# The last phase of a split-fp32 matrix product rewritten as a second Strassen step over pairs of samples, with part of its sums on GpSimd

## The reference, cut to what matters

```
y   = conv1d(x, weight, groups=4, pad=4) + (cond @ c_weight.T)[:, :, None] + bias   # x: (32, 128, 2048)
out = x + y @ kernel + ffn_bias                                                     # kernel: 2048 x 2048
        + B_eff (A_eff y) + B_shared (A_shared y)                                   # rank 32 each, mixed by gate
```

## Time and profile before

| | us |
|---|---|
| median of 3 runs | 1692.22 |
| lowest and highest | 1692.02, 1692.98 |
| the profiled execution's own time | 1692.59 |
| its span in the profile | 1690.8 |
| PE busy in it | 1680.7 (99%) |
| DVE busy | 1092.4 (65%) |
| ACT busy | 681.5 (40%) |
| POOL busy | 36.7 (2%) |

### The profile page before, as it was taken

The page is one execution under the profiler, slowest core; times in us unless marked ns, Lnnn a source line. Parts: engine busy times, 40 slices in busy tenths (PEclk is TensorE's granted clock), DMA queues, the critical chain, the costliest instruction groups (busy, mean ns, idle before and its releaser), DMA issues.

```text
span 1690.8 us, 21782 instructions
## 1 busy us (share of the span) xinstructions
PE 1680.7 (99%) x8432; PEld 1437.2 (85%) x8432; DVE 1092.4 (65%) x1501; ACT 681.5 (40%) x862; POOL 36.7 (2%) x70
## 2 busy tenths in 40 slices
PE   9999999999999999999999999999999999999998
PEld 6799998888888898888998888888888888888887
DVE  7888888965454689999986344455555545464443
ACT  7776776744222665566642112232233111121110
POOL 0011111110000000000000000000000000000000
PEclk9999999999999999999999999999999999999999
DMA  8978777976666667777666665577676898886764
GB/s 253 282 229 291 254 240 257 325 251 220 224 211 222 207 225 276 275 266 264 245 234 246 221 223 199 197 230 250 229 230 220 306 331 299 309 314 241 261 234 153
DMA packets 180287, 420.25 MB, mean 249 GB/s; under 512 B 50740, under 2 KB 90260, under 8 KB 175544
## 3 DMA queue, kind: packets, MB, share of 16 engines
q1 hardware_dynamic: 169960, 380.95, 65.9%
q0 software_dynamic: 9216, 33.56, 5.6%
q10 hardware_dynamic: 1008, 4.34, 0.9%
HBM read 272.76 MB, written 146.03 MB: 248 GB/s over the span
## 4 chain that ended last, share of the span: by engine, by line
PE 97%; DVE 2%; ACT 0%; DMA 0%; issue 0%; DVEq 0%
PE acc L1518 71%; PE cps L1387 15%; PE cps L1437 4%; PE acc L1421 3%; PE acc L1354 2%; PE acc L1471 1%; PE cps L1447 0%; DVE w_lo L975 0%; DVE x_q L986 0%; PE cps L1457 0%; PE acc L1493 0%; DMA st<-in_L_ffn_kernel 0%; DVE g L1012 0%; PE cps L1455 0%; DVE g L1003 0%
## 5 line engine op out<-in xcount | busy, mean ns | idle before, releaser
L1518 PE MATMUL acc<-w_hi,y_t 128*128 128x512 f32 x3584 | 991.7, 390 | 2.0 <-issue 1.0
L1518 PEld LDWEIGHTS acc<-w_hi,y_t 128*128 128x128 f32 x3584 | 665.3, 188 | 136.6 <-issue 2.1
L1518 PE MATMUL acc<-w_lo,y_t 128*128 128x512 f32 x1792 | 552.9, 390 | 0.0
L1518 PEld LDWEIGHTS acc<-w_lo,y_t 128*128 128x128 f32 x1792 | 336.3, 188 | 71.5
L713 ACT COPY x_q<-x_raw 32x512 f32<-32x512 f32 x248 | 269.6, 1087 | 21.1 <-DVE x_lo L993 13.4
L1387 PE MATMUL cps<-cw,x_hi 128*128 128x256 f32 (+2 forms) x1088 | 243.9, 312 | 0.4 <-DVE x_lo L1172 0.4
L752 ACT CAST y_t<-g 128x1024 fp32r<-128x1024 f32 x95 | 100.2, 1054 | 331.7 <-PE acc L1518 298.2
L1113 DVE TENSOR_TENSOR g<-acc,g 128x1024 f32<-128x1024 f32 x96 | 117.3, 1223 | 163.8 <-PE acc L1421 114.3
L1073 DVE TENSOR_TENSOR y_t<-g,y_t 128x1024 fp32r<-128x1024 f32 x95 | 116.1, 1222 | 102.0 <-ACT y_t L752 101.7
L1387 PE MATMUL cps<-cw,x_lo 128*128 128x384 f32 (+2 forms) x768 | 180.9, 283 | 0.0
L1387 PEld LDWEIGHTS cps<-cw,x_hi 128*128 128x128 f32 x1088 | 176.4, 189 | 3.6 <-DVE x_lo L1172 1.2
(11 more groups left out here) (127 smaller groups left out, 1006.6 us busy)
## 6 DMA issues: line engine op xcount, KB each, us to landing
g<-A SPq DMA_DIRECT2D x80, 512.0 KB, 4.7
g<-U SPq DMA_DIRECT2D x80, 512.0 KB, 6.2
A<-g SPq DMA_DIRECT2D x64, 512.0 KB, 4.6
g<-in_x SPq DMA_DIRECT2D x64, 512.0 KB, 6.2
out<-g SPq DMA_DIRECT2D x64, 512.0 KB, 3.5
x_raw<-in_x SPq DMA_DIRECT2D x31, 1024.0 KB, 5.2
U<-g SPq DMA_DIRECT2D x48, 512.0 KB, 4.1
g<-in_L_ffn_kernel POOLq DMA_DIRECT2D x32, 512.0 KB, 6.5
```

Of the source, the lines that this page charges most:

```text
L1518: ins = T.matmul(acc[:, b, m, :], y_buf[b][:, c, part, :], wt[:, k % SLOTS, m * 512:(m + 1) * 512], start=(c == 0 and part == 0 and wt is ...
```

## The change

Phase 6 is no longer 16 units but 8 passes over two pairs each (`one_pass`). In a pass the two units' products, 2 x (128 x 1024) by 1024 x 1024, are taken as one 2 x 2 block product, with the halves of K (512) as inner blocks and the halves of the columns (512) as outer ones, by a second Strassen-Winograd step: seven products of 128 x 512 by 512 x 512, each 12 matmuls (4 chunks by 3 split products) into one PSUM bank. The low-rank part is 2 matmuls for each of the four output blocks. A pass has 84 + 8 matmuls, where two units have 96 + 8.

- The weight of phase 6 (B22) becomes seven 512 x 512 blocks (14 tiles of 128 x 1024 where there were 8), three of them quarters of B22 and four formed from them: GpSimd loads B22, does 16 additions of 128 x 512 and stores `V4` to `V7` after the last convolution, in phase 3. The 14 tiles use `w_hi`/`w_lo` slots and the memory of `x_hi`, `x_lo` and `cw`, which nothing else uses by then. Six are split in phase 5, one in every one or two units, the other eight in its last unit and in the first pass.
- The seven left operands are a11, a12, a22 and four sums of the two samples' halves (`pass_sums`, four DVE instructions). Each is split apart (`hi_part`, `lo_part`, 128 x 512), in five buffers `y_part`.
- Of the products, P1 and P5 are copied out by ACT (`pass_copy`), P6 and P7 are added to running sums by DVE (`pass_us`), and GpSimd adds these four to the output tile: six additions of 128 x 512. GpSimd also does what `pre_add` did, two additions of 128 x 1024 (`pass_residual`). DVE adds the four banks that hold only their own block (`pass_add`), and SP stores each block of 256 KB apart.
- DMA issues of a pass are in another order (below). Unit 95, the last of phase 5, has its own low-rank part inside it, after chunk 6.

The core of the diff:

```diff
+EV_P1, EV_P2, EV_P6, EV_L11, EV_P5, EV_P7, EV_L22, EV_P3, EV_L12, EV_P4, EV_L21 = range(1, 12)
+EVS = 11
+EV_OF = (EV_P1, EV_P2, EV_P6, EV_P5, EV_P7, EV_P3, EV_P4)
+SUMS = (("E1", 0, 0), ("U2", 0, 1), ("P5", 0, 1), ("P5", 1, 1), ("U3", 1, 1), ("U3", 1, 0))
+SUMS_E1, SUMS_U2, SUMS_P5, SUMS_P5B, SUMS_U3B, SUMS_U3 = range(1, 7)
+ADDS = ((EV_L11, 0, 0, SUMS_E1), (EV_L22, 1, 1, SUMS_U3B), (EV_L12, 0, 1, SUMS_P5), (EV_L21, 1, 0, SUMS_U3))
+NADD = len(ADDS)
...
+        pair_w = [(w_hi[:, k], w_lo[:, k]) for k in (4, 5, 6)] + [
+            (xh_flat[:, k * HALF:(k + 1) * HALF], xl_flat[:, k * HALF:(k + 1) * HALF]) for k in range(2)] + [
+            (cw_flat[:, 0:HALF], cw_flat[:, HALF:2 * HALF])] + [(w_hi[:, k], w_lo[:, k]) for k in (7, 8, 9, 10, 0, 1, 2, 3)]
+        y_part = [cw_flat[:, 2 * HALF:3 * HALF].rearrange("p (c h o) -> p c h o", h=2, o=P)] + [
+            y_t[:, b, h * 4:(h + 1) * 4] for b in range(2) for h in range(2)]
...
+        part_src = [y_in_buf[0][:, 0:512], y_in_buf[0][:, 512:HALF], s_two, s_one, s_one, s_two,
+                    y_in_buf[1][:, 512:HALF]]
+        V1, V3 = B22[0:4][:, :, 0:512], B22[4:8][:, :, 512:HALF]
+        V2 = B22[4:8][:, :, 0:512]
+        PAIR_SRC = [V1, V2, V6_d, V5_d, V7_d, V3, V4_d]
+        pass_bank = {EV_P1: cps[:, 0, :], EV_L11: cps[:, 1, :], EV_P6: cps[:, 2, :], EV_P5: cps[:, 3, :],
+                     EV_P7: acc[:, 0, 0, :], EV_L22: acc[:, 0, 1, :], EV_L12: acc[:, 1, 0, :], EV_L21: acc[:, 1, 1, :]}
+        pass_out = [[g[:, 6], g[:, 0]], [g[:, 7], g[:, 1]]]
...
+            def load_pass_out(q, j):
+                u = QU + 2 * q + j
+                p = u % NP
+                if q == 0:
+                    sp.wait_ge(pre_added, lora_index(u) - 1)
+                else:
+                    sp.wait_ge(pass_pre, 2 * (q - 1) + j + 1)
+                sp.dma_start(xres[j], x[2 * p][:, HALF:L]).then_inc(xres_in[j], 16)
+                if q >= 2:
+                    sp.wait_ge(stage_out[j], 16 * (QU // 2) + 32 * (q - 1))
+                elif j == 0:
+                    sp.wait_ge(stage_out[q], 16 * (QU // 2))
+                else:
+                    sp.wait_ge(u4_out[q], 16 * (NP // 2))
+                sp.wait_ge(u4_out[p % 2], 16 * (p // 2 + 1))
+                sp.dma_start(pass_out[q % 2][j], U4_d[p]).then_inc(stage_in[j], 16)
+            def load_pass_y(u):
+                q, j = divmod(u - QU, 2)
+                if j == 0:
+                    sp.wait_ge(sums_ready, 4 * q)
+                    sp.wait_ge(y_lo_ready, QU + 7 * (q - 1) + 2)
+                else:
+                    sp.wait_ge(y_lo_ready, QU + 7 * q)
+                sp.dma_start(y_in_buf[j], A12_d[u % NP]).then_inc(y_in[j], 16)
+                sp.wait_ge(diff_ready, diff_index(u) - 1)
+                sp.dma_start(other[j], S2_d[u % NP]).then_inc(other_in[j], 16)
+            def store_pass(q, n):
+                j, h = ADDS[n][1:3]
+                sp.wait_ge(pass_added, NADD * q + n + 1)
+                sp.dma_start(out[2 * (2 * q + j)][:, HALF + h * 512:HALF + (h + 1) * 512],
+                             pass_out[q % 2][j][:, h * 512:(h + 1) * 512]).then_inc(stage_out[j], 16)
...
+            load_b(QU)
+            for j in range(2):
+                load_pair(10 + j)
+                load_pass_out(0, j)
+            for q in range(QS):
+                u = QU + 2 * q
+                if q >= 1:
+                    store_pass(q - 1, 3)
+                if q + 1 < QS:
+                    load_pass_y(u + 2)
+                for j in range(2):
+                    if q == 0:
+                        sp.wait_ge(lora_done, lora_index(u + j) - 1)
+                    else:
+                        sp.wait_ge(pass_ev, EVS * (q - 1) + (EV_L12, EV_L21)[j])
+                    sp.wait_ge(axd_out, 16 * NP)
+                    sp.dma_start(ax_words[:, j], axs_d[(u + j) % NP]).then_inc(axs_in[j], 16)
+                if q == 0:
+                    for n in (12, 13):
+                        load_pair(n)
+                    sp.wait_ge(evac_u, NP)
+                    sp.dma_start(U4_d[NP - 1], u2_buf[1]).then_inc(u4_out[1], 16)
+                    store_stage(QU - 1)
+                if q + 1 < QS:
+                    for j in range(2):
+                        load_pass_out(q + 1, j)
+                    load_pass_y(u + 3)
+                store_pass(q, 0)
+                if q + 1 < QS:
+                    load_b(u + 2)
+                store_pass(q, 1)
+                store_pass(q, 2)
+            store_pass(QS - 1, 3)
...
+            def pass_residual(q):
+                for j in range(2):
+                    pool.wait_ge(stage_in[j], 16 * ((QU + 2 * q + j - NP) // 2 + 1))
+                    pool.wait_ge(xres_in[j], 16 * (lora_index(QU + 2 * q + j) // 2 + 1))
+                    V.tensor_tensor(pass_out[q % 2][j], pass_out[q % 2][j], xres[j], ALU.add).then_inc(pass_pre, 1)
+            pass_residual(0)
+            for q in range(QS):
+                for n, (what, j, h) in enumerate(SUMS):
+                    half = pass_out[q % 2][j][:, h * 512:(h + 1) * 512]
+                    if what in ("E1", "P5"):
+                        pool.wait_ge(pass_copied, 2 * q + (1 if what == "E1" else 2))
+                    else:
+                        pool.wait_ge(pass_u, 2 * q + (1 if what == "U2" else 2))
+                    if n == 0:
+                        pool.wait_ge(pass_pre, 2 * q + 2)
+                    else:
+                        pool.wait_ge(pass_summed, len(SUMS) * q + n)
+                    V.tensor_tensor(half, half, pass_sum_buf[what], ALU.add).then_inc(pass_summed, 1)
+                if q + 1 < QS:
+                    pass_residual(q + 1)
...
+            hi_part(0)
+            split_pair(6)
+            hi_part(1)
+            split_pair(7)
+            hi_part(2)
+            split_pair(8)
+            for q in range(QS):
+                n = 7 * q
+                b_split(QU + 2 * q)
+                if q == 0:
+                    hi_part(3)
+                    split_pair(9)
+                hi_part(n + 4)
+                pass_copy(q, "E1")
+                if q == 0:
+                    split_pair(10)
+                    split_pair(11)
+                hi_part(n + 5)
+                if q == 0:
+                    split_pair(12)
+                    split_pair(13)
+                hi_part(n + 6)
+                if q + 1 < QS:
+                    hi_part(n + 7)
+                pass_copy(q, "P5")
+                if q + 1 < QS:
+                    for i in range(8, 11):
+                        hi_part(n + i)
...
+            lo_part(0)
+            split_pair(6)
+            lo_part(1)
+            difference(QU + 1)
+            pass_sums(0, 0)
+            split_pair(7)
+            lo_part(2)
+            pass_sums(0, 1)
+            pre_add(QU - 1)
+            split_pair(8)
+            for q in range(QS):
+                n, u = 7 * q, QU + 2 * q
+                more = q + 1 < QS
+                if q >= 1:
+                    pass_add(q - 1, 3)
+                b_split(u)
+                if q == 0:
+                    lo_part(3)
+                    pass_sums(0, 2)
+                    split_pair(9)
+                lo_part(n + 4)
+                if q == 0:
+                    split_pair(10)
+                    split_pair(11)
+                    evac_u4(QU - 1)
+                lo_part(n + 5)
+                if q == 0:
+                    split_pair(12)
+                    split_pair(13)
+                lo_part(n + 6)
+                if more:
+                    difference(u + 2)
+                pass_us(q, "U2")
+                if q == 0:
+                    evac(QU - 1)
+                pass_add(q, 0)
+                if more:
+                    lo_part(n + 7)
+                    lo_part(n + 8)
+                    difference(u + 3)
+                pass_us(q, "U3")
+                if more:
+                    pass_sums(q + 1, 0)
+                    lo_part(n + 9)
+                    pass_sums(q + 1, 1)
+                pass_add(q, 1)
+                if more:
+                    lo_part(n + 10)
+                    pass_sums(q + 1, 2)
+                pass_add(q, 2)
+            pass_add(QS - 1, 3)
...
+            def pass_product(q, i, ev, joined=False):
+                n = 7 * q + i
+                pe.wait_ge(y_lo_ready, QU + n + 1)
+                for c in range(NCH // 2):
+                    k = 2 * i + c // 2
+                    if q == 0:
+                        pe.wait_ge(w_lo_ready, NCH * 6 + k + 1)
+                    cols = slice(c % 2 * 512, (c % 2 + 1) * 512)
+                    for part, h in ((0, 0), (0, 1), (1, 0)):
+                        ins = T.matmul(pass_bank[ev], y_part[n % YS][:, c, part, :], pair_w[k][h][:, cols],
+                                       start=(c == 0 and part == 0 and h == 0),
```

(45 more changed lines are left out.)

191 lines of the change are left out of this document (164 added, 27 removed).

## The result

The changed kernel takes 1751.25 us (median of 4 runs, 1749.84 to 1752.48), the kernel before beside it 1692.31 (4 runs): a ratio of 1.0347 with a 95% interval of 1.0329 to 1.0365, slower by 59 us. The profiled execution took 1751.03. The forecast was slower by 33 us, at 1725; the range ended at 1752.

A forecast was written before the change was run, and what follows sets the result against it. PE's instruction stream at its pace was taken as the bound: 1692.6 - 21.8 (matmuls) - 1.2 (shorter end) + 36 (new PE waits) + 19 (GpSimd contention) = 1724.6, said as 1725 us; range 1699 to 1752.

The forecast's parts named there:

- What is saved: Phase 6: 96 matmuls fewer, 21.8 us; one bank in a row costs nothing; the end 1.2 us shorter.
- The loop of a pass: Phase 6: SP's loads and DVE's list take 24.1 us a pass; PE, needing 20.9, waits 3.2 at the low-rank operand.
- DVE's wait for S2: Sign in phase 6 that the forecast is right: DVE waits for the DMA of S2 at the second difference.
- The hand-over: Phase 5 into the passes: PE waits of 4.2, 2.8, 6.4 and 7.7 us, together 21.
- rival (1): Passes of phase 6: no contention between GpSimd and DVE, 1706 us; chance 0.25.
- GpSimd's part: Passes of phase 6: GpSimd's additions lengthen DVE's list by contention, 2.4 us a pass, 19 us in all.
- Half done on average, and I take that: Phase 6: a DVE instruction meets a running POOL one half done; 2.4 of 4.8 us a pass is paid.
- Rival (2): Passes of phase 6: full exclusion of DVE and POOL, loop longer by 4.8 us, 38 in all, 1744; chance 0.22 with longer.
- or longer: Case of full exclusion in the passes or a still longer time; chance 0.22 together.
- The prediction's estimate from that page: GpSimd additions in the passes: 2.5 us for 1024 columns, 1.2 for 512; with full exclusion 7.4 us a pass.
- Rival (3): Phase 6: SP's queue is no loop, PE never waits in a steady pass, only the hand-over remains; 1679 us, chance 0.11.
- Elsewhere: Phases 3 and 5: forming and splitting the new weights costs nothing, 2 us if a load comes late in phase 3.

The follow-up runs named there:

- TensorE kept at work: Changed kernel plus 24 unread matmuls before the low-rank part of each pass from the second on: 1751.5 us.
- the operand first: Changed kernel with the low-rank operands loaded ahead of A12 and S2, the first also ahead of the previous pass's last store: 1750.03 us.
- small additions: Changed kernel with GpSimd's additions in the passes cut to 8 columns each, waits and signals kept, output incomplete: 1712.25 us.
- the other order: Changed kernel with low-rank operands, then the second sample's A12 and S2, loaded earlier: 1730.54 us; with GpSimd's additions also cut to 8 columns: 1685.46 us.
- the version that beats both: Rewritten SP and DVE lists, all additions on VectorE, plus earlier low-rank operand loads and residual additions at the hand-over: 1687.06 us, 0.9961 of the kernel before.

## Why the prediction was right or wrong

**What is saved: right.** 96 matmuls went, and 12 into one bank in a row cost nothing: the blocks of the changed kernel take 2.73 us, 0.2275 each. The end is shorter by 0.9 us, not 1.2: DVE's 0.69 and 2.9 us of store (1745.61 to 1749.2), for 1.23 and 3.2.

**The loop of a pass: right.** Without GpSimd's weight a pass takes 24.3 us, 24.1 predicted, and the second S2 lands 16.4 us after the head, 16.6 predicted. The wait stands where it was put, at the low-rank matmuls; at 5.6 to 6.7 us in the steady passes, which last 29.8 us, longer than the 24 to 28 given. The prediction didn't see that PE closes a loop of the same length: operand, two low-rank and 12 other matmuls at half clock, ACT's copy, DVE's list. In the changed kernel S2 lands at 1623.43 and the second difference starts at 1624.17, so DVE's wait for S2 there, a sign that the prediction named, shows only with TensorE kept at work (3.00 us). Taking PE's way out (the operand first, TensorE at work) changed nothing that stands out of the scatter of single runs (1750.03 and 1751.5 for 1751.25).

**The hand-over: right.** Predicted 4.2, 2.8, 6.4 and 7.7 us; the four waits are 4.73, 2.48, 5.99 and 9.59, and with small additions 6.03, 1.98, 6.43 and 5.85. With small additions they add up to 20.3 us for the 21 predicted, and the single ones are off by up to 1.9. (The terms of all waits in the prediction make 37.3 us, not 37.5; nothing hangs on it.)

**What was left out: the clock.** The forecast counted waits alone. With small additions PE's waits in phase 6 add up to 30.6 us, 36 predicted; by the forecast's own sum that makes 1692.6 - 23 + 30.6 = 1700, and the kernel takes 1712.25. From PE's first matmul of the passes to its last end go 210.0 us there (1496.8 to 1706.8), 42.9 more than 167.1, so 12.3 of them aren't waits. 45 matmuls start over 0.3 us after the one before and lose 8.8 us, nearly all of it behind the waits of 3.8 to 6.4 us, at the lower clock. The other 3.5 are not put down to anything. The 6 us between rival (1)'s 1706 and 1712 are thus about 12 that were left out, less 5 of waits that were too many.

**GpSimd's part: the step that failed.** It was put at 19 us and measured 39.0 (1751.25 for 1712.25); with the 6 us just told these are the 26 us between 1725 and 1751.25. Two numbers in it were too small.

- The length. From memset and affine select came 0.83 us for 512 columns and 1.57 for 1024. Measured: 1.28 for 512 columns, and 2.83 in the mean for 1024, part of which is waiting for DVE (the shortest of any run is 2.53). An instruction with one input was no row for one with two.
- The share. "Half done on average, and I take that", 2.4 us a pass. DVE's list lasts 13.4 us for 7.4, and the pass 29.8 for 24.3: 5.5 to 6 us a pass, 39 us in all for 19. The middle was picked between two ends that mean different mechanisms, and no row pointed to it. DVE doesn't meet an addition halfway on average: POOL's next one gets going as DVE's instruction ends, so that L1248 loses 2.0 us of its 2.71 and the L1229 behind it 1.6 of 2.29.

Four instructions grew: L1244 (1.67 us, POOL's L868 beside it), L1229 (0.96), L1248 (2.71) and L1229 (2.29), 7.6 us for 4 x 0.61: 5.2 of the 6 in the kernel with TensorE kept at work. In the changed kernel the second difference grew as well, to 2.31 us. Rival (2) let DVE wait for the whole length of the additions that this list meets; it was the mechanism that came true. Its price, 38 us for 39.0, is right by two errors that cancel: by the measured lengths the four additions take 2 x 1.28 and 2 x 2.53 us or more, 7.6 for its 4.8, and DVE's list grew by 6, since part of them runs beside instructions that read PSUM and where DVE is idle. Its 1744 is 7 us low, 6 of them the clock's part above. The measured time lies in its case ("or longer"), outside the forecast's own range of 1712 to 1738, and inside the wide one by 0.75 us: direction, place and loop of the loss were worked out, and that the time is still in the range owes something to luck.

The rule of the Trainium skill (SBUF — State Buffer, "Who interferes with whom") that the two exclude each other for a whole instruction is what the rows show: 2.71 us for 0.69 with two SBUF inputs, 0.68 with one in PSUM. By its GPSIMD Engine Reference (3.1) the additions were to take about twice DVE's time; 1.28 to 0.69 and 2.83 to 1.23 are 1.9 and 2.3 times, the second with POOL's waiting in it. The prediction's estimate from that page, 7.4 us a pass by both pages together, is above the 5.5 to 6 measured.

**Rival (3)**, the loads are no loop, is false for the lists as written. Its pass without waits is real all the same: the other order reaches it with GpSimd's additions cut down, 21.1 us. **Elsewhere:** PE's waits ahead of phase 6 grew by 1.8 us, inside the 0 to 2 given. 0.8 of them stand in phase 3, at 920.5 us, for an instruction of DVE (L1380) that lasts 1.50 us beside one of the 16 additions that form the weights, and 0.41 beside none; these take 24.5 us in all, not 13.

Open: why the version that beats both has passes of 21.8 us, where a pass without waits takes 21.1 with the new order and small additions; waits of 0.1 to 0.8 us a pass are recorded, and the rest isn't settled. How a GpSimd instruction with one input shares with DVE was not tried.

## What to carry to other kernels

Work that is moved to GpSimd need not be taken off VectorE where both read two tiles in SBUF: here eight additions a pass lengthened VectorE's list by 5.5 to 6 us, as much as it needs to do them itself (6 x 0.61 + 2 x 1.15), and with its own additions the kernel was 33 us faster. Where a bound of a price has two ends that stand for two mechanisms, weigh the mechanisms and take one, not the middle, and test the lengths on a row of the same kind of instruction. And before a stage on TensorE is cut, walk once around the ring of the queues that feed it, first transfer to last instruction: it was 24 us here for 20.9 on TensorE, it could be computed from the profile before, and a second ring behind it was as long.
